# A two-layer recurrent kernel: the delta-input product written to PSUM, one more buffer in each ring, results added on TensorE and the order of ScalarE's work changed

## What is computed

```python
o = (o - mu) / jnp.sqrt(var + 1e-05) * ln_g + ln_b       # end of layer 0
return o * gate @ Wo.T
...
x_and_res = x @ in_proj_w                                # layer 1, each row
h = silu(conv(xp) + conv_b)
x_dbl = h @ x_proj_w
dlt, Bm, Cm = (x_dbl[..., :dt_rank], x_dbl[..., dt_rank:dt_rank + n], x_dbl[..., dt_rank + n:])
delta = jax.nn.softplus(dlt @ dt_proj_w + dt_proj_b)
deltaA = jnp.exp(jnp.einsum('bld,dn->bldn', delta, A))
deltaB_u = (delta * h)[..., None] * Bm[:, :, None, :]
def step(state, t):
    dA_t, dBu_t, c_t = t
    state = dA_t * state + dBu_t
    y_t = jnp.einsum('bdn,bn->bd', state, c_t)
    return (state, y_t)
...
y = ys.transpose(1, 0, 2) + h * D_param
y = y * _silu(res)
return y @ out_proj_w
```

## Time and profile before

| | |
|---|---|
| median of three runs | 1348.35 us (1345.88 to 1348.6) |
| profiled execution | 1351.8 us, its span 1350.0 us |
| DVE busy | 1223.7 us, 91% of the span |
| TensorE busy | 988.6 us, 73% |
| ACT, POOL busy | 713.1 and 713.7 us, 53% each |
| granted TensorE clock, mean | 0.864 of full |
| attention steps 28 to 31 | 649.0 to 720.4 us of the span |
| join and dispatch | 720.4 to 802.2 us |
| rows 0 to 7 | 802.2 to about 1330 us |

### The profile page before, as it was taken

How to read it: one execution, slowest core, us unless ns; L and a number is a source line. 1 busy time by engine, 2 the same in 40 slices (tenths; PEclk the granted TensorE clock), 3 DMA queues, 4 the chain that set the end, 5 groups by cost and what they waited for, 6 DMA issues and landing times. The chain is left out here.

```text
span 1350.0 us, 15880 instructions
## 1 busy us (share of the span) xinstructions
PE 988.6 (73%) x3622; PEld 574.5 (43%) x3623; DVE 1223.7 (91%) x2295; ACT 713.1 (53%) x1345; POOL 713.7 (53%) x651
## 2 busy tenths in 40 slices
PE   3765347887877877887625776768888888888874
PEld 2412335555555655555524622233444344444331
DVE  7988799999999999999998789999979698979799
ACT  5644015555556555555323264456666666766751
POOL 5038732333333333333210036888888789888895
PEclk9887558899899898898756598789999899999898
DMA  9739141000000000000432033464444344444346
GB/s 306 212 107 306 58 137 37 19 24 19 20 23 22 20 22 19 20 22 14 125 128 78 16 126 103 144 168 162 155 153 148 143 158 165 155 161 145 123 160 188
DMA packets 106770, 145.48 MB, mean 108 GB/s; under 512 B 26347, under 2 KB 82424, under 8 KB 101856
## 3 DMA queue, kind: packets, MB, share of 16 engines
q1 hardware_dynamic: 90816, 114.51, 26.8%
q0 software_dynamic: 10240, 25.32, 5.8%
q10 hardware_dynamic: 5664, 5.11, 1.3%
HBM read 112.26 MB, written 39.04 MB: 112 GB/s over the span
## 5 line engine op out<-in xcount | busy, mean ns | idle before, releaser
L2092 DVE TENSOR_TENSOR ps<-ps,cv 128x512 f32<-128x512 f32 x256 | 163.1, 683 | 21.5 <-ACT ps L1619 20.1
L1139 PE MATMUL ps<-Q,ident 128*128 128x512 f32 x256 | 139.2, 636 | 32.9 <-issue 9.8
L836 POOL TENSOR_TENSOR Q<-LR,xn 128x512 f32<-128x512 f32 x96 | 122.5, 1276 | 29.1 <-PE ps L1139 14.4
L978 PE MATMUL ps<-wd_a,xn 128*128 x576 | 94.6, 314 | 42.4 <-ACT xn L1350 42.4
L1368 ACT ACTIVATE x<-x 128x128 f32<-128x128 f32 (+1 forms) x127 | 32.2, 278 | 150.6 <-DVE x L1921 67.0
L767 POOL DMA_INDIRECT y_tok<-xnT,meta x72 | 72.5, 1007 | 62.1 <-ACT xnT L1356 49.3
L958 PE MATMUL ps<-wg_a,xnT 128*128 x144 | 92.7, 730 | 17.0 <-issue 10.7
L978 PEld LDWEIGHTS ps<-wd_a,xn 128*128 128x128 f32 x576 | 79.7, 214 | 56.4 <-issue 54.9
L988 PE MATMUL ps<-x,ident 128*128 128x64 f32 x512 | 74.0, 297 | 30.4 <-DMA wu_a<-in_wu_a 15.3
L745 POOL DMA_INDIRECT slots_x<-xn,sl_put x64 | 74.6, 1166 | 40.5 <-DVE sl_put L1753 21.3
L776 POOL TENSOR_TENSOR xn<-xn 128x512 f32<-128x512 f32 x24 | 30.3, 1264 | 120.5 <-DVE x L1915 95.5
(11 more groups left out here) (349 smaller groups left out, 2769.2 us busy)
## 6 DMA issues: line engine op xcount, KB each, us to landing
cv<-bc_scr SPq DMA_DIRECT2D x64, 512.0 KB
xn<-bc_scr SPq DMA_DIRECT2D x24, 1024.0 KB
O<-bc_scr SPq DMA_DIRECT2D x8, 1024.0 KB
slots_x<-O POOLq DMA_DIRECT2D x28, 260.0 KB, 5.6
qkv_scr<-wg_a SPq DMA_DIRECT2D x24, 256.0 KB
xnT<-slots_x SPq DMA_DIRECT2D x72, 64.0 KB
x<-in_x SPq DMA_DIRECT2D x8, 512.0 KB, 5.8
y_tok<-slots_x SPq DMA_DIRECT2D x2, 2048.0 KB, 13.4
```

What stands on the lines that cost most here:

```text
L836: pool.tensor_tensor(yc_g0[:, n % 4, :], st_g0[:, n % 2, :], cn, ALU.mult).then_inc(yc_ready, 1)
L978: m = pe.matmul(ps[:, 0, 0:D], hidT[:, k, f * P:(f + 1) * P], wd_a[:, bass.ds(off + f * D, D)], start=(f == 0), stop=(f == FC - 1))
L1139: pe.matmul(ps[:, 4, :], ident[:], yc_g0[:, n % 4, :], start=(n == 0), stop=(n == NS - 1)).then_inc(y0_used, 1)
L2092: tt(dBu(g), ps[:, 2 + g, :], b_rows[:, n % 4, :], ALU.mult).then_inc((inject0, b_used)[g], 1)
```

## The change

In the rows, `delta_h` moves from POOL to the end of DVE's row and writes its product straight to PSUM; ScalarE's copy of it is gone. The state rings get a third buffer, `yc` a fifth, `yo` a fourth, from space that the product had held. `finish` stands before the scans of state 3 instead of behind those of state 2. On ScalarE the log of the softplus moves behind the decays of the next state, and the two `taps1` behind the next row's first decays (g 0) and into the next row (g 1). POOL's `delta_sum` moves one state later.

In the join, TensorE adds the expert results (two matmuls with the identity for each group, `mix_sum`) in attention steps 29 and 30, and ScalarE takes the silu from PSUM within step 30; `oT_scale` moves to step 31. The normalisation's four instructions for each group move from DVE to ScalarE (`norm_group`), for which DVE makes a bias. `add_group` is split in `attended` and `residual`.

```diff
+        mix_bank = (3, 4, 5, 6, 1, 2, 0, 3)
+        nbias1 = nrm[:, 1, 0:NT]
...
-        h1, res1, del1, dh1 = ([r.take(GD, L) for r in even_odd] for _ in range(4))
+        h1, res1, del1 = ([r.take(GD, L) for r in even_odd] for _ in range(3))
+        more = even_odd[1].take(2, L)
...
+        yo_g1 = yo_g1[:, 0, :], yo_g1[:, 1, :], flat(seg[:])[:, 0:L], more[:, 0, :]
+        yc_ring = tuple(yc_g0[:, i, :] for i in range(4)) + (more[:, 1, :],)
+        st_rings = (st_g0[:, 0, :], st_g0[:, 1, :], st_g0_more), (st_g1[:, 0, :], st_g1[:, 1, :], st_g1_more)
...
@@ pool
-            def delta_h(r, s, g):
-                pool.wait_ge(delta_ready, r * GD + (g + 1))
-                pool.tensor_tensor(dh1[s][:, g, :], del1[s][:, g, :], h1[s][:, g, :], ALU.mult).then_inc(dh_made, 1)
...
                         for g in range(GD):
                             delta_sum(1, 1, g)
-                        for g in range(GD):
-                            delta_h(1, 1, g)
...
-                    pool.wait_ge(y0_used, c * NS + (n - 3))
+                    pool.wait_ge(y0_used, c * NS + (n - 4))
...
-                        pool.wait_ge(y1_used, units_before(c) + u - 2)
+                        pool.wait_ge(y1_used, units_before(c) + u - 3)
...
-                    if n in (10, 11) and c < LAST:
-                        delta_sum(c + 1, 1 - s, n - 10)
-                    if n in (12, 13) and c < LAST:
-                        delta_h(c + 1, 1 - s, n - 12)
+                    if n in (11, 12) and c < LAST:
+                        delta_sum(c + 1, 1 - s, n - 11)
@@ tensor
+            def mix_sum(g):
+
+                if g == 5:
+                    pe.wait_ge(o_var, 1)
+                if g == 7:
+                    pe.wait_ge(mix_silu, 1)
+                y2 = xnT[:].rearrange("p (i c) -> p i c", c=D)
+                pe.matmul(ps[:, mix_bank[g], :], ident[:], xn[:, 4 * g:4 * g + 4, :], start=True, stop=False)
+                pe.matmul(ps[:, mix_bank[g], :], ident[:], y2[:, 4 * g:4 * g + 4, :], start=False, stop=True).then_inc(mix_ps, 1)
...
-            for c in range(AFTER + 1, NCH - 1):
-                step(c, False)
+            for c, gs in ((AFTER + 1, range(4)), (AFTER + 2, range(4, G4))):
+                q_sums(c, 0, HD)
+                pe.wait_ge(y_loaded, 16 * 8)
+                for g in gs:
+                    mix_sum(g)
+                o_sums(c)
@@ scalar
-            step(AFTER + 2, False, early=decay_rates, late=lambda: oT_scale(range(6)))
-            step(NCH - 1, False, last=True)
+            def mix_silus(gs):
+                act.preload_act_table(ACT.Silu)
+                for g in gs:
+                    act.wait_ge(mix_ps, g + 1)
+                    act.activation(xn[:, 4 * g:4 * g + 4, :], ps[:, mix_bank[g], :].rearrange("p (i c) -> p i c", c=D), ACT.Silu).then_inc(mix_silu, 1)
+                act.preload_act_table(ACT.Exp)
+
+            def first_mixes():
+                decay_rates()
+                mix_silus(range(4))
+
+            step(AFTER + 2, False, early=first_mixes, late=lambda: mix_silus(range(4, G4)))
+            step(NCH - 1, False, last=True, early=lambda: oT_scale(range(6)))
...
+            def norm_group(g):
+                act.wait_ge(ln_bias1, g + 1)
+                for i in group_tiles(g):
+                    act.activation(xn[:, i, :], x[:, i, :], ACT.Identity, scale=rstd[:, i:i + 1], bias=nbias1[:, i:i + 1]).then_inc(xn_ready, 1)
...
                             softplus_parts(r, t, 1)
                             softplus_exp(r, t)
+                        if n == 10:
                             softplus_log(r, t)
-                    if c < LAST and n == NS - 1:
-                        for g in range(GD):
-                            dh_copy(r, t, g)
-                    if r2 < B and n in (13, 15):
-                        taps1(r2, s, n // 15)
+                    if r2 < B and n == 14:
+                        taps1(r2, s, 0)
+                    if c and r < B and n == 0:
+                        taps1(r, t, 1)
@@ vector
-                for i in group_tiles(g):
-                    dve.tensor_scalar(xn[:, i, :], x[:, i, :], mv[:, i, 0:1], rstd[:, i:i + 1], ALU.subtract, ALU.mult).then_inc(xn_ready, 1)
+                dve.scalar_tensor_tensor(by_group(nbias1.unsqueeze(2), g), by_group(mv[:], g)[:, :, 0:1], -1.0, v, ALU.mult, ALU.mult).then_inc(ln_bias1, 1)
...
-            for g in range(3):
-                combine(g)
             o_centre(1)
-            for g in range(3, G4):
-                combine(g)
+            attended(0)
+            attended(1)
             o_var_of(1)
...
             def delta_h(r, s, g):
                 dve.wait_ge(delta_ready, r * GD + (g + 1))
-                tt(dh1[s][:, g, :], del1[s][:, g, :], h1[s][:, g, :], ALU.mult).then_inc(dh_made, 1)
+                since(dve, (inject0, b_used)[g], r * NS)
+                tt(ps[:, 2 + g, :], del1[s][:, g, :], h1[s][:, g, :], ALU.mult).then_inc(dh_ready, 1)
...
-                    if c or n >= 2:
-                        dve.wait_ge(*product(c, g, n - 2))
+                    if c or n >= 3:
+                        dve.wait_ge(*product(c, g, n - 3))
...
+                    if n == 3 and c:
+                        finish(c - 1, t)
                     scan(n, 0)
                     scan(n, 1)
-                    if n == 2 and c:
-                        finish(c - 1, t)
                 if own(c):
                     own_products(NS - 1)
+                if r < B:
+                    for g in range(GD):
+                        delta_h(r, t, g)
```

100 lines of the change are left out of this document (52 added, 48 removed).

## The result

| | before | changed |
|---|---|---|
| median | 1347.77 us (1345.88 to 1349.03, 6 runs) | 1336.01 us (1330.75 to 1337.26, 6 runs) |
| profiled execution, its span | 1351.8, 1350.0 us | 1332.28, 1330.5 us |
| ratio to before | | 0.9907, 95% interval 0.9891 to 0.9924 |

What follows compares the result with a forecast made beforehand. DVE was taken to bound the join and, with TensorE a close second and DVE's waits between, the rows. The terms summed to -14.5 us, from 1348.35 to 1333.9 on the median's scale, so 1334 us; range 1318 to 1347.

Steps and rivals of the forecast that it cites:

- Row ends, the wait that goes: Row starts: DVE's waits for ScalarE's copy of the delta_h product all vanish, -20.1 us.
- The work that comes: Seven row ends: DVE gains a pair of product instructions, 1.27 us for each pair, +8.9 us.
- The port: Ends of rows 1 to 6: delta_h, both inputs in SBUF, waits for POOL's gaps, two microseconds each, +12 us.
- Row 0: First row: POOL's multiplications and additions halve, so DVE's stall shrinks from 4.88 to about 2.4 us, -2.5 us.
- The softplus: State 12, four rows: decays come 3.7 us earlier, ahead of the log; 5.5 of 13.5 us waiting stay, -8.
- Late next: State 14, six rows: TensorE's second inner waits for the first taps1, 0 to +18 us, taken as +4.
- rival 2: Rows 2 to 6: TensorE sets the pace, not below some 62 us each; time 1344 us, chance 0.23.
- Rings: Rows: more buffers cut DVE's waits for POOL's products, at most 5.6 us, taken as -3.
- the join: Before the rows: normalisation on ScalarE brings the router's logits at 771.3 instead of 774.72, -3.4 us, bounds 0 and -7.9.
- Steps 29 to 31: Attention: added matmuls, silus and moved scalings fit idle time at full clock, 0; at half clock up to +5 us.
- the forecast's case: Whole kernel: time between 1328 and 1341 us, chance 0.45.
- rival 1: Row ends: POOL yields sooner, DVE's 12 us of waiting become 0 to 7.6; time 1322 to 1329 us, chance 0.20.

Runs made afterwards that it cites:

- rival 1's condition: Changed kernel, but delta_h at the ends of rows 1 to 6 reads its first operand from PSUM instead of SBUF (wrong numbers): 1336.81 us, ratio 0.9845.
- the kernel with both cuts: Changed kernel with most of the experts' arithmetic left out on TensorE and delta_h's first operand read from PSUM: 1305.25 us, ratio 0.9622.

## Why the prediction was right, and where it was not

- **Row ends, the wait that goes** (-20.1): right. No wait for a copy is left, and with the product back on POOL 30.2 us of them return.
- **The work that comes** (+8.9): right; seven pairs cost 1.20 us each from start to start, +8.4.
- **The port** (+12): right in mechanism and size, 11.0. The lengths depend on where POOL stands, 1.30 in row 0 where no multiplication was running, 4.08 where two followed. The chosen two microseconds for each of six ends came out at 1.8, but they were chosen, between bounds of 0 and 34.8; and with the product alone moved the waiting was 4.3.
- **Row 0** (-2.5): the clash of 5.56 us became 1.86, so -3.7; with a disturbance of 2.3 us that the row of before had and this one did not, and the extra pair of products, row 0 is 4.9 us shorter.
- **The softplus** (-8): this step failed. Of the 5.8 us at state 12 of row 3, 5.56 remained; at states 12 and 13 of rows 2 to 6 15.4 us stand where 15.1 stood, and the waits for decays rose by 2.3 us over all. With the log back at state 9 the time was the same. The step took the list of ScalarE as the only thing that makes decays late, and let a wait at state 12 vanish because the decays moved by 3.7 us. The two table loads and the log stayed on ScalarE's list, ahead of state 13's decays; and the time saved elsewhere brought DVE sooner to decays whose place TensorE's pace sets. Of the 5.5 us that the step let stay, its own rule gives 2.4 (2.1 of the 5.8 and 0.3 of the 4.0); for the rest, at state 13, it gives no working. With TensorE's load cut, 6.3 us stayed.
- **Late next** (+4): wrong in mechanism. It let TensorE wait at `inner` for the first `taps1`; in rows 1 to 7 TensorE's matmuls waited for it once, for 0.4 us, and with `taps1` back in its old place the time was the same. What came late were decays and B's rows from DMA. Together with the softplus the term was put at -4; measured are +2.3 on decays and +2.2 on B's rows, +4.5. This is rival 2's mechanism at a smaller size: rows 3 and 5 stayed at 68.2 and 67.1 us against 67.0 and 67.7 before.
- **Rings** (-3): the waits for products went entirely, -5.6; `finish` (-1.2) -2.2. Both were mis-sized low, but the run with short rings shows that the rings' part is no saving: without the longer rings the pairs are 7.0 us shorter instead.
- **Row 0's start** (-1.2) and **the join** (-3.4): -1.24 and -3.65. Followed, the logits were put at 771.3; they came at 768.57, or 771.1 with the 2.5 us added that lie before the change. The order of events was as written, ScalarE's eight normalisations last.
- **Steps 29 to 31** (0): right; the bound at full clock held, though half of step 29's sums ran at the lower level: the idle time had room for that, and the step's output sums still waited 0.64 us for POOL.
- The terms found in the profile sum to -14.9 us: -20.1 + 8.4 + 11.0 - 3.7 - 2.3 + 2.3 + 2.2 - 5.6 - 2.2 - 1.24 - 3.65. Another -2.1 in rows 1 to 7 I cannot name, and -2.5 lie before the change. The forecast's nearness to 1336.0 thus rests on a softplus term that was 8 to 10 us too hopeful and on rings, `finish` and row 0 that were 7 us too cautious.
- Luck has a part in it. The sum was made from the profiled execution, and between profiled executions the change was -19.5, not -14.5; between medians it was -11.8 here and -22.4 on another chip. The forecast lies between the three. (Rows 1 to 7 took 445.0 us before, not the 447 that the prediction names; no term rests on that.)

The chances stood well for the forecast's case, but rival 2 was not as separate from it as it was written: TensorE's pace does not forbid the gain, it takes back what is added to it. That is why the port's 11 us, the term on which rival 1 rested, would have been worth nothing: with rival 1's condition, tried, rows 1 to 7 took 437.5 us against 437.8, and the time was 2 us above that of a kernel with the port's waits on the same chip. (By its ratio alone, 0.9845, it would stand within rival 1's 1322 to 1329; but so would that kernel, with 0.9843.)

The Trainium skill, "SBUF — State Buffer", "SBUF: two separate sides", says that whichever of DVE and GpSimd starts first gets the shared pair for the whole instruction. In row 3 the second product waited while two POOL multiplications went by, and in the earlier trace rows four; there the trace does not agree with a wait of only one. At the end of row 1 it does: DVE got in between two. That a DVE instruction with at most one SBUF input does not contend, as the same page says in "Who interferes with whom", the trace agrees with: 1.27 or 1.28 us in all twelve pairs with an operand in PSUM.

## What to carry to other kernels

A wait is booked on the engine that released it, but the cause may stand further back: ScalarE's decays were late since an expert's piece ahead of them in its list waited for TensorE. Before an edit is costed in such a stretch, look for the window in which an engine has no gap at all; what is saved elsewhere comes back as a wait there, and edits that each remove a wait (a port's, a table load's, a ring's) do not add up. And where the same code differs by 8 us in one stage and by 12 in its median from chip to chip, a part's worth can be read only against a kernel beside it on the same chip, and even then roughly. Take the heavy engine's load away for one run: it shows which savings are real and held back, and which were none.

## What the runs showed of the hardware

- A DVE `tensor_tensor` with both inputs in SBUF that became ready as POOL multiplied waited in most cases until POOL had a gap: 0.2 to 1.1 us behind one instruction, up to 2.8 behind two (3.46 us instead of 0.68) and 4.9 behind four. At the end of row 1 it got in between two, in eight executions alike, and the second of them took 1.72 us instead of 1.27. When it does and when not is open. A POOL scatter beside it cost it nothing (0.69 us in row 0, 0.71 in row 3).
- Executions of the same code differ by 8 us in rows 1 to 7 (434.0 and 441.9), together with TensorE's granted clock (1.00 against 0.95 in the two rows concerned). Behind a rest of 3.42 us it was at 0.50 for the next eight matmuls, which took 4.64 us instead of 2.42.
- Row 0 differs too: 76.4 and 83.6 us in the two profiled executions of the changed kernel, 76.4 to 91.1 over all fourteen. There TensorE stood for up to 25 us at the product for delta, with nothing that the profile shows to wait for, then ScalarE and DVE behind it, while POOL was sending out tokens. From the kernel with both cuts:

```profile
856.86 2.07 PE L1154 MATMUL ps<-V,wg_a 64*128 64x512 f32 x2 [25.36 <-issue]
```

```profile
855.54 0.69 ACT L1594 ACTIVATE V<-ps,wg_a 128x512 f32<-128x512 f32 x1 [25.32 <-remote]
```

```profile
859.78 0.69 DVE L2144 TENSOR_TENSOR seg<-Q,O 128x512 f32<-128x512 f32 x1 [9.47 <-remote]
```

  It came in kernels with either form of the rows. What it waits for is open; a difference of less than some 10 us between two single profiled executions is no evidence in this kernel, and the row-by-row lengths above are to be read with that.
